# Graph layer on one core: the weighting of the key one-hots on DVE, with the chunk index innermost in its result

## What is computed

```python
def _denoise_gcn_layer(x, row, col, noise, nbW, nbb, selfW, selfb, attW, attb):
    h1 = jax.nn.relu(x[row] @ nbW + nbb)
    h2 = jax.nn.relu(x[col] @ selfW + selfb)
    log_alpha = jnp.concatenate([h1, h2], axis=1) @ attW + attb
    u = jnp.clip(noise, EPS_NOISE, 1.0 - EPS_NOISE)
    gate = jax.nn.sigmoid(jnp.log(u) - jnp.log1p(-u) + log_alpha)
    mask = jnp.clip(gate * (ZETA - GAMMA) + GAMMA, 0.0, 1.0)[:, 0]
    rowsum = jax.ops.segment_sum(mask, row, num_segments=N_NODES) + EPS_DEG
    d_inv_sqrt = jnp.clip(rowsum ** (-0.5), 0.0, 10.0)
    vals = mask * d_inv_sqrt[row] * d_inv_sqrt[col]
    return jax.ops.segment_sum(vals[:, None] * x[col], row, num_segments=N_NODES)

h = jnp.maximum(_layernorm(x, axis=-1), 0.0)
x1 = layer(h, ...); x2 = layer(x1, ...)
return x + h + x1 + x2
```

## Time and profile before

| | us |
|---|---|
| median of 3 runs | 6730.72 (6729.32 to 6736.85) |
| the profiled execution: its own time | 6725.77 |
| its span in the profile | 6723.7 |
| mask stage of layer 0 in it, from the first L1130 to L1551 | 834 |
| DVE busy over the whole span | 5556.7 (83%) |
| PE busy | 4115.6 (61%) |
| ACT busy | 2500.0 (37%) |
| POOL busy | 2252.7 (34%) |

### The profile page before, as it was taken

One profiled execution on the slowest core, in us unless ns is written; L12 is line 12 of the kernel. 1 busy time (PEld: TensorE's weight loads), 2 busy tenths in 40 slices (PEclk: granted clock), 3 DMA queues, 4 the chain that ended last, 5 costly groups with the idle time before them and its releaser, 6 DMA issues. The chain is left out here.

```text
span 6723.7 us, 166891 instructions
## 1 busy us (share of the span) xinstructions
PE 4115.6 (61%) x58388; PEld 3656.1 (54%) x58388; DVE 5556.7 (83%) x10207; ACT 2500.0 (37%) x5126; POOL 2252.7 (34%) x1874
## 2 busy tenths in 40 slices
PE   3777777765855555355557777855555255557666
PEld 2666666654545554344556676555554245446666
DVE  8999999995399999899966665099999899976666
ACT  2656566642344443355510001344443255520000
POOL 0000000000089998000025453089998000024444
PEclk9777777765555555677778888555555576768888
DMA  2000000002365654799979986165554799989888
GB/s 64 0 0 0 0 0 0 0 1 15 69 204 194 197 196 150 240 332 333 332 241 246 244 245 179 41 198 199 197 196 146 239 331 332 332 249 246 240 247 230
DMA packets 438059, 1160.67 MB, mean 173 GB/s; under 512 B 211241, under 2 KB 216974, under 8 KB 437402
## 3 DMA queue, kind: packets, MB, share of 16 engines
q1 hardware_dynamic: 316671, 549.99, 26.5%
q0 software_dynamic: 75264, 354.33, 19.5%
q10 hardware_dynamic: 46036, 255.30, 10.0%
...
## 5 line engine op out<-in xcount | busy, mean ns | idle before, releaser
L582 POOL DMA_INDIRECT work<-msg_d,widx x444 | 552.5, 1244 | 2075.1 <-issue 1620.4
L1577 PE MATMUL psG<-y_window,area 128*128 128x64 bf16 x14976 | 686.1, 219 | 764.4 <-DVE area L1225 595.9
L1577 PEld LDWEIGHTS psG<-y_window,area 128*128 128x128 bf16 x14976 | 642.2, 116 | 808.6 <-issue 501.5
L1590 PE MATMUL psG<-work,edge 112*128 112x192 bf16 x7104 | 794.3, 282 | 393.3 <-DVE edge L1260 392.8
L1590 PEld LDWEIGHTS psG<-work,edge 112*128 112x128 bf16 x7104 | 750.9, 151 | 436.3 <-DVE edge L1260 357.1
L638 ACT ACTIVATE work<-iota,work 128x149 bf16<-128x149 f32 x2496 | 788.9, 406 | 0.0
L1399 PE MATMUL psG<-area,work 128*128 128x112 bf16 x2496 | 551.0, 390 | 339.1 <-DVE area L967 339.1
L1399 PEld LDWEIGHTS psG<-area,work 128*128 128x128 bf16 x2496 | 357.6, 148 | 487.5 <-issue 344.0
L1392 PE MATMUL psG<-work,merge 128*128 128x148 bf16 x4992 | 542.8, 293 | 69.8 <-ACT work L638 69.8
L1392 PEld LDWEIGHTS psG<-work,merge 128*128 128x128 bf16 x4992 | 526.1, 131 | 92.3 <-issue 66.2
L745 ACT ACTIVATE edge<-merge,npid 128x2048 bf16<-128x2048 uint16 x156 | 312.4, 2003 | 705.3 <-DMA merge<-crel_d 705.3
...
...
## 6 DMA issues: line engine op xcount, KB each, us to landing
msg_d<-work ACTq DMA_DIRECT2D x312, 784.0 KB, 4.7
area<-rlo_d SPq DMA_DIRECT2D x312, 512.0 KB, 4.4
merge<-crel_d SPq DMA_DIRECT2D x312, 512.0 KB, 5.4
area<-crelp_d SPq DMA_DIRECT2D x312, 512.0 KB, 5.8
y_window<-y_d SPq DMA_DIRECT2D x312, 48.0 KB, 3.7
...
```

The costliest lines, as they stand in the source:

```text
L582: pool.indirect_dma_start(out=windows[par][0:WP, g, :, :].rearrange("p s w -> p (s w)"), out_offset=None, in_=msg_d, in_offset=bass.Indire ...
L1577: ins = pe.matmul(psG[:, 2 * h + k // CH, k % CH * D:(k % CH + 1) * D], col_one_hots[:, h, k * P:(k + 1) * P], y_window[:, h, m * D:(m + 1 ...
L1590: ins = pe.matmul(psG[:, slot_, 0:MW], q_one_hots[slot_][0:WP, g, :, s], windows[slot_][0:WP, g, s, 0:MW], start=g == 0 and s == 0, stop=g ...
```

## The change

POOL stops after the three parts: it counts the last one in a new semaphore `mask_split`, and `mask_parts` is now held twice (index `v`), with the part as the outer index and the edge innermost. DVE has a new function `weigh_rows`, which does what L567 did, for pair `p_ - 1` at the start of the turn of pair `p_`, ahead of `hots(p_+2)`. `weighted` has its indices in the order part, column, chunk, so the chunk is innermost, as in `h_hot`; PE's moving operand for chunk k is then 72 values 16 elements (32 bytes) apart. `h_hots` no longer waits for `weighted_ready`; POOL waits for it instead, before it overwrites `mask_parts` of two pairs ago. The first turn of the loop is written out, and the weighting of the last pair follows the loop. Some buffers in `scratch` are moved to make room.

```diff
--- before.py
+++ after.py
@@ -198,11 +198,11 @@
         crel_bc = flat_merge.bitcast(u16).rearrange("p (u e) -> p u e", u=2)
         q_bc = bcast[:, :, :].rearrange("p a e -> p (a e)").rearrange("p (u e) -> p u e", u=2)
         h_hot = scratch[:, 0:2 * HW * CT].bitcast(bf16).rearrange("p (v u n j) -> p v u n j", v=2, u=2, j=CT)
-        weighted = [t.rearrange("p (u j m n) -> p u j m n", u=2, j=CT, m=3) for t in (scratch[:, 800:800 + 3 * HW * CT].bitcast(bf16), far[:, 12000:12000 + 6 * HW * CT])]
-        mask_parts = scratch[:, 1960:1960 + 3 * CT].bitcast(bf16).rearrange("p (e m) -> p e m", m=3)
-        mask_rest = scratch[:, 2020:2020 + 2 * CT]
-        mask_now = scratch[:, 2130:2130 + 2 * CT]
-        gate = scratch[:, 2060:2060 + 4 * CT].rearrange("p (v e) -> p v e", v=2)
+        weighted = [t.rearrange("p (u m n j) -> p u m n j", u=2, j=CT, m=3) for t in (scratch[:, 800:800 + 3 * HW * CT].bitcast(bf16), far[:, 12000:12000 + 6 * HW * CT])]
+        mask_parts = scratch[:, 1952:1952 + 6 * CT].bitcast(bf16).rearrange("p (m v e) -> p m v e", m=3, v=2)
+        mask_rest = scratch[:, 2050:2050 + 2 * CT]
+        mask_now = scratch[:, 2150:2150 + 2 * CT]
+        gate = scratch[:, 2084:2084 + 4 * CT].rearrange("p (v e) -> p v e", v=2)
         q_hot = [t[:, 4 * ST // 2:8 * ST // 2].bitcast(bf16).rearrange("p (v u e) -> p v u e", v=2, u=2) for t in (cur, work)]
         lo_hot = [t[:, 0:4 * ST // 2].bitcast(bf16).rearrange("p (v u n k) -> p v u n k", v=2, u=2, k=CT) for t in (cur, work)]
         junk = [t.rearrange("p (k n) -> p k n", k=CH) for t in (flat_merge[:, 0:CH * HI], scratch[:, 0:CH * HI])]
@@ -264,7 +264,7 @@
         y_ready, y_stored = sem("y_ready"), sem("y_stored")
         weighted_by_act, weighted_by_dve = sem("weighted_by_act"), sem("weighted_by_dve")
         dist_ready, logits_ready, sigmoid_ready, general_step = (sem(n) for n in ("dist_ready", "logits_ready", "sigmoid_ready", "general_step"))
-        odd_hot_ready, extras_ready, gate_ready, parts_step, weighted_ready, row_sums_kept = (sem(n) for n in ("odd_hot_ready", "extras_ready", "gate_ready", "parts_step", "weighted_ready", "row_sums_kept"))
+        odd_hot_ready, extras_ready, gate_ready, parts_step, weighted_ready, row_sums_kept, mask_split = (sem(n) for n in ("odd_hot_ready", "extras_ready", "gate_ready", "parts_step", "weighted_ready", "row_sums_kept", "mask_split"))
         mask_turn, mask_turn_kept, mask_stored, mask_loaded, row_lane_loaded, lane_columns_stored = (sem(n) for n in ("mask_turn", "mask_turn_kept", "mask_stored", "mask_loaded", "row_lane_loaded", "lane_columns_stored"))
         span_ready, widest_ready, local_ready, b_ready, b_stored = (sem(n) for n in ("span_ready", "widest_ready", "local_ready", "b_ready", "b_stored"))
         lo_loaded, crel_loaded, msg_index_loaded, y_window_loaded = ([sem(f"{n}{h}") for h in range(2)] for n in ("lo_loaded", "crel_loaded", "msg_index_loaded", "y_window_loaded"))
@@ -547,7 +547,7 @@
                     for v in range(2):
                         p_ = i * 2 + v
                         cols = bass.ds(p_ * 2 * CT, 2 * CT)
-                        done = (L * TP + p_) * 5
+                        done = (L * TP + p_) * 4
 
                         def step(n, ins):
                             ins.then_inc(parts_step, 1)
@@ -557,15 +557,13 @@
                         pool.nop(nofuse=True)
                         step(1, pool.tensor_scalar(mask_now[:, :], gate[:, v, :], 1.0, None, ALU.min))
                         pool.tensor_copy(ga[:, cols], mask_now[:, :]).then_inc(mask_ready, 1)
-                        step(2, pool.tensor_copy(mask_parts[:, :, 0], mask_now[:, :]))
-                        step(3, pool.tensor_tensor(mask_rest, mask_now[:, :], mask_parts[:, :, 0], ALU.subtract))
-                        step(4, pool.tensor_copy(mask_parts[:, :, 1], mask_rest))
-                        step(5, pool.tensor_tensor(mask_parts[:, :, 2], mask_rest, mask_parts[:, :, 1], ALU.subtract))
-                        for u in range(2):
-                            wait(pool, sums_added, L * T + p_ * 2 + u - 3)
-                            pool.nop(nofuse=True)
-                            pool.tensor_tensor(weighted[v][:, u, :, :, :], h_hot[:, v, u, :, :].rearrange("p n j -> p j n").unsqueeze(2).to_broadcast([P, CT, 3, HW]),
-                                               mask_parts[:, u * CT:(u + 1) * CT, :].unsqueeze(3).to_broadcast([P, CT, 3, HW]), ALU.mult).then_inc(weighted_ready, 1)
+                        wait(pool, weighted_ready, L * T + p_ * 2 - 2)
+                        pool.nop(nofuse=True)
+                        step(2, pool.tensor_copy(mask_parts[:, 0, v, :], mask_now[:, :]))
+                        step(3, pool.tensor_tensor(mask_rest, mask_now[:, :], mask_parts[:, 0, v, :], ALU.subtract))
+                        step(4, pool.tensor_copy(mask_parts[:, 1, v, :], mask_rest))
+                        pool.tensor_tensor(mask_parts[:, 2, v, :], mask_rest, mask_parts[:, 1, v, :], ALU.subtract).then_inc(mask_split, 1)
+
                 with pool.If(is_local):
                     steps(pool, 0, T // 4, split_masks)
                 with pool.Else():
@@ -1120,7 +1118,6 @@
                     dve.tensor_scalar(col_hot[:, v, 0, :], crel_bc[:, 0, :], pid[:, 0:1], None, ALU.is_equal).then_inc(one_hot_ready[1], 1)
 
                 def h_hots(p_, v):
-                    wait(dve, weighted_ready, L * T + p_ * 2 - 2)
                     dve.tensor_tensor(h_hot[:, v, :, :, :], hwin[:, :, :].unsqueeze(1).to_broadcast([P, 2, HW, CT]),
                                       hb[:, bass.ds(p_ * 2 * CT, 2 * CT)].rearrange("p (u j) -> p u j", u=2).unsqueeze(2).to_broadcast([P, 2, HW, CT]), ALU.is_equal).then_inc(hi_one_hot_ready, 1)
 
@@ -1141,9 +1138,18 @@
                         dve.tensor_tensor(lo_hot[L][:, v, u, :, :], iota16[:, :, :],
                                           lof[:, bass.ds(t * CT, CT)].unsqueeze(1).to_broadcast([P, P, CT]), ALU.is_equal).then_inc(lo_one_hot_ready, 1)
 
+                def weigh_rows(p_, v):
+                    dve.wait_ge(mask_split, L * TP + p_ + 1)
+                    for u in range(2):
+                        wait(dve, sums_added, L * T + p_ * 2 + u - 3)
+                        dve.tensor_tensor(weighted[v][:, u, :, :, :], h_hot[:, v, u, :, :].unsqueeze(1).to_broadcast([P, 3, HW, CT]),
+                                          mask_parts[:, :, v, u * CT:(u + 1) * CT].unsqueeze(2).to_broadcast([P, 3, HW, CT]), ALU.mult).then_inc(weighted_ready, 1)
+
                 def local_masks(i):
                     for v in range(2):
                         p_ = i * 2 + v
+                        if not isinstance(i, int) or p_ > 0:
+                            weigh_rows(p_ - 1, 1 - v)
                         if not isinstance(i, int) or p_ + 2 < TP:
                             hots(p_ + 2, v)
                         choose(p_, v)
@@ -1180,7 +1186,9 @@
                     for v in range(2):
                         hots(v, v)
                     h_hots(0, 0)
-                    steps(dve, 0, T // 4, local_masks)
+                    local_masks(0)
+                    steps(dve, 1, T // 4, local_masks)
+                    weigh_rows(TP - 1, 1)
                     dve.wait_ge(row_sums_ready, L + 1)
                     dve.tensor_reduce(abr[:, 0, :], psR[:, 1, 0:3 * HI].rearrange("p (m h) -> p h m", m=3), AX.X, ALU.add).then_inc(row_sums_kept, 1)
                 with dve.Else():
@@ -1521,7 +1529,7 @@
                         pe.wait_ge(weighted_ready, L * T + t + 1)
                         for k in range(CT):
                             ins = pe.matmul(psR[:, 1, 0:3 * HI].rearrange("p (m h) -> p m h", m=3)[:, :, FIRST[k]:FIRST[k] + HW],
-                                            lo_hot[L][:, v, u, :, k], weighted[v][:, u, k, :, :], start=False, stop=False)
+                                            lo_hot[L][:, v, u, :, k], weighted[v][:, u, :, :, k], start=False, stop=False)
                         ins.then_inc(sums_added, 1)
 
                 def local_masks(i):
```

## The result

The changed kernel takes 6635.64 us in the median of four runs (6625.63 to 6648.75), the kernel before 6730.02 in the same comparison: a ratio of 0.9863 (95% interval 0.9839 to 0.9887), 94 us less. The forecast was 77 less, 6654. The profiled execution took 6641.64 us with a span of 6639.7, 84 under the span before; layer 0's mask stage, from the first `choose` to the closing matmul, takes 788.9 us and not 834.1, layer 1's 789.8 and not 835.4, and the rest of the two spans differs by 7 us the other way.

A forecast was written before the change was run, and what follows sets the result against it. Bound: a serial chain of DVE and POOL excluding each other, 10.64 us a pair. Rounds -37.7, front +4.9 and end -5.5 give -38.3 a layer, -77 for two: 6730.7 - 77 = 6654 us, range 6620 to 6690.

The forecast's parts named there:

- What bounds the kernel before: Mask stage: DVE's two-input instructions and POOL's hold each other up, a serial chain of 10.64 us a pair.
- What goes: POOL loses L567, 5.40 us of its own work a pair; DVE's stalls in L1141 go, 3.4 us a pair.
- What comes on DVE: Weighting: two instructions of 1152 bf16 values at 755 ns each, 1.36 us together.
- The new chain: From L1135's end over ACT's sigmoid and POOL's split: DVE weighs 4.12 us after it, a new wait of some 1.4 us.
- PE: add_rows with 32-byte steps: 142 ns a matmul, 2.3 us a tile in place of 1.2, staying hidden.
- the pair: One round of the mask stage: 4.12 + 1.36 + 4.7, with 0.02 for register steps, 10.2 us against 10.64.
- Layer 0's front: Start of the mask stage: DVE waits for the first split, so the second pair's L1135 ends 4.9 us later.
- POOL shut out: Rival, chance 0.12: POOL's small steps wait until DVE stands still; 11.0 us a pair, time near 6773.
- One value at a time: Rival, chance 0.05: DVE's weighting reads one value at a time, not two; 11.4 us a pair, 6833.
- PE as the bound: Rival, chance 0.07: at 3.5 us a tile matmuls and gather set 10.7 us a pair; time near 6733.
- The fourth one-hot: Rival, chance 0.06: ACT's odd_hot, waiting for its own broadcast, sets 10.75 us a pair; near 6737.
- A shorter chain: Rival, chance 0.08: POOL's steps end by 3.3 us after L1135; 9.4 us a pair, 6536.

## Why the prediction was right

- **What bounds the kernel before**, a serial chain and not DVE's work: right. The layout alone on POOL shows it apart: 0.68 us off POOL's two, 0.70 off the pair.
- **What goes.** L567 left POOL, and `lo_hots` fell to a median of 1218 ns (said: 1216 in the mean; it was 1223).
- **What comes on DVE**: 755 ns forecast from L1124 and L967; 755 measured in 140 instructions. The doubling that was a rival was the truth of the other layout, at three times: 2.26 us.
- **The new chain**: the steps after R were forecast at 1.27, 2.36, 2.83 and 4.01 us and came at 1.28, 2.35, 2.83 and 3.95. The weighting came at 3.99 (4.10 in every other pair) and not at 4.12. Its wait was forecast at about 1.4 us and 210 in all; it was 206.6.
- **PE**: 142 ns a matmul forecast from L1399; 4.62 / 32 = 144 measured, and no one waits for it. The Trainium skill, "SBUF — State Buffer", section "Door 1: The DMA port swizzle", says that accesses to new 16-byte lines are penalised; the trace agrees, 144 ns against 75 and against 69 in the kernel with contiguous reads (2.20 / 32). The Trainium skill's "VectorE: DVE Perf Modes", in the section on the TRN2 errata, has no such term and would leave PE at its old time by its formula; the measurement decides against it.
- **The term that was mis-sized** is the pair: 10.2 forecast, 10.10 measured. I took 0.1 us for the semaphore from POOL to DVE, which is 0.03 to 0.04, and 0.385 for the spacing of POOL's steps, the last of which is 0.35 (2204.60 to 2204.95). Against it, in every other pair 0.11 us more lie between POOL's last step and the weighting (0.15 and not 0.03). In nearly all of these DVE's queue does a register operation of 65 ns after the wait for `mask_split` and before L1145 (2215.26 to 2215.33), and in none of the others. The loop's branch is no part of it, for that was done at 2210.96. Over 76 rounds that is -45.0 and not -37.7. That layer 1 could be counted like layer 0 came out by luck: its front cost 2.8 us and not 5.8, and its rounds gave 42.4 and not 45.0, which nearly cancel. Layer 0's front cost 5.8 and not 4.9: L743, waiting for its broadcast, started 0.3 us after L1132 had started and not 1.6 before (1853.06 and 1852.74; 1851.85 and 1853.40 before the change), and `gates` is behind it on ACT. Of these 1.9 us POOL gave back 0.9, since its steps ran free there. The end gave 5.9, for 5.5.
- **The rivals.** POOL shut out: no, the minimum and the copy were done inside DVE's row of three, and the first cast 0.07 us after it. One value at a time: no. PE as the bound: no, 10 to 16 us from a slower `choose` and a longer last pair, and nothing from a wait in the rounds. The fourth one-hot: no, by the pair of 9.02 with `hots` first; its loop was also not as the prediction has it, since the issue followed `hots` and not L747 (0.7 us after L747's end in the kernel before, in the median). A shorter chain, 9.4 a pair: not here, and even with the copy out of the chain it is 9.66 to 9.79.
- **What I did not see.** I named DVE's own sum of 8.9 us, and that the weighting waits ahead of `hots`, but not that one swap of two calls would take nearly all of the difference. Nor did I price the layout on POOL, which is half of the diff and by itself is worth at least as much as the whole.

What stays open: why a few of the broadcasts take over 7 us to land, and why the front of layer 1 costs less than that of layer 0.
